# Cross-attention over 98 tiles of keys: the weighted sums of a tile in two groups of four matmuls

## What is computed

```python
lat = layernorm(latents, ...); ctx = layernorm(context, ...)
q = lat @ Wq; k, v = split(ctx @ Wkv)            # 16 heads of 64
attn = clip(einsum("bhnd,bhsd->bhns", q, k) * 64 ** -0.5, -11, 11)
attn = softmax(attn)
out = einsum("bhns,bhsd->bhnd", attn, v) @ Wo + bo
x = x + out
```

## Time and profile before

| | us |
|---|---|
| median of 3 runs | 1075.84 (1074.86 to 1076.63) |
| profiled execution, device time | 1071.72 |
| its span, first to last instruction | 1070.0 |
| PE busy | 1059.8 (99%) |
| PEld busy | 901.2 (84%) |
| DVE busy | 928.6 (87%) |
| ACT busy | 660.9 (62%) |
| POOL busy | 173.0 (16%) |
| chain that ended last | PE 97%, DVE 2% |

### The profile page before, as it was taken

How to read it: one execution, slowest core, us unless ns; L and a number is a source line. 1 busy time by engine, 2 the same in 40 slices (tenths; PEclk the granted TensorE clock), 3 DMA queues, 4 the chain that set the end, 5 groups by cost and what they waited for, 6 DMA issues and landing times.

```text
span 1070.0 us, 18208 instructions
## 1 busy us (share of the span) xinstructions
PE 1059.8 (99%) x5494; PEld 901.2 (84%) x5494; DVE 928.6 (87%) x1326; ACT 660.9 (62%) x934; POOL 173.0 (16%) x213
## 2 busy tenths in 40 slices
PE   9999999999999999999999999999999999999997
PEld 7888888888888888888888888888888888888876
DVE  4999999999999999989888888888888888888875
ACT  4666666666666666656666666666666666666642
POOL 3233232232332332312000000000000000000000
PEclk9999999999999999999999999999999999999998
DMA  5321221222212212231151111111111111111000
GB/s 202 94 73 51 74 65 58 74 51 71 74 49 74 74 49 74 62 98 43 50 124 34 40 44 30 44 44 30 44 44 29 44 43 30 44 30 31 1 1 6
DMA packets 52509, 58.78 MB, mean 55 GB/s; under 512 B 31170, under 2 KB 32772, under 8 KB 52356
## 3 DMA queue, kind: packets, MB, share of 16 engines
q1 hardware_dynamic: 52052, 57.80, 18.7%
q10 hardware_dynamic: 432, 0.66, 0.2%
HBM read 58.20 MB, written 0.13 MB: 55 GB/s over the span
## 4 chain that ended last, share of the span: by engine, by line
PE 97%; DVE 2%; ACT 0%; issue 0%; POOL 0%; DVEq 0%; POOLq 0%
PE wide L457 25%; PE wide L458 25%; PE wide L459 25%; PE wide L498 17%; PE wide L521 1%; PE wide L528 1%; PE wide L535 1%; PE wide L550 0%; PE wide L556 0%; PE wide L543 0%; PE wide L508 0%; PE wide L747 0%; DVE a_max L1222 0%; PE wide L680 0%; PE wide L685 0%
## 5 line engine op out<-in xcount | busy, mean ns | idle before, releaser
L819 ACT ACTIVATE ex<-wide,c_rstd 128x512 f32<-128x512 f32 x392 | 270.3, 689 | 200.7 <-PE wide L459 199.8
L457 PE MATMUL wide<-qk_hi,d_hi 128*128 128x512 f32 x784 | 305.2, 389 | 0.0
L459 PE MATMUL wide<-qk_hi,d_lo 128*128 128x512 f32 x784 | 305.1, 389 | 0.0
L458 PE MATMUL wide<-qk_lo,d_hi 128*128 128x512 f32 x784 | 305.0, 389 | 0.0
L1028 DVE TENSOR_TENSOR ph<-ex,ph 128x1024 fp32r<-128x1024 f32 x195 | 238.9, 1225 | 71.3 <-ACT ph L826 71.1
L826 ACT CAST ph<-ex 128x1024 fp32r<-128x1024 f32 x195 | 205.4, 1053 | 150.1 <-DVE ex L1003 150.1
L1037 DVE TENSOR_TENSOR den_all<-den_all,ex 128x1024 f32<-128x1024 f32 x193 | 234.7, 1216 | 0.0
L498 PEld LDWEIGHTS wide<-ph,vhl 128*128 128x128 f32 x1568 | 212.6, 190 | 16.7 <-DVE ph L1028 2.1
L498 PE MATMUL wide<-ph,vhl 128*128 128x256 f32 x1568 | 219.0, 282 | 0.0
L457 PEld LDWEIGHTS wide<-qk_hi,d_hi 128*128 128x128 f32 x784 | 147.2, 188 | 31.8 <-DVE qk_lo L1042 0.3
L459 PEld LDWEIGHTS wide<-qk_hi,d_lo 128*128 128x128 f32 x784 | 147.1, 188 | 30.6
(11 more groups left out here) (156 smaller groups left out, 628.5 us busy)
## 6 DMA issues: line engine op xcount, KB each, us to landing
t_all<-in_ctxT_dram SPq DMA_DIRECT2D x98, 384.0 KB, 3.1
x_pair<-in_ctx_dram SPq DMA_DIRECT2D x49, 256.0 KB, 2.7
diff<-sig_all SPq DMA_DIRECT2D x194, 0.5 KB, 1.9
wkv<-in_Wo_dram SPq DMA_DIRECT2D x2, 1024.0 KB, 10.0
wq<-in_Wq_dram SPq DMA_DIRECT2D x2, 512.0 KB, 7.3
wkv<-in_Wv_dram SPq DMA_DIRECT2D x2, 512.0 KB, 6.1
wkv<-in_Wk_dram ACTq DMA_DIRECT2D x1, 512.0 KB, 4.7
wkv<-in_Wk_dram SPq DMA_DIRECT2D x1, 512.0 KB, 10.2
```

The costliest lines, as they stand in the source:

```text
L457: pe.matmul(dst, hi, mhi, start=start, stop=False)
L458: pe.matmul(dst, hi, mlo, start=False, stop=False)
L459: return pe.matmul(dst, lo, mhi, start=False, stop=stop)
L819: act.activation(ex[b][:, c * HC:(c + 1) * HC, :], sc_bank[c][:, :].rearrange("p (h q) -> p h q", h=HC), ACT.Exp, scale=c_rstd[s4][:, b:b ...
```

## The change

`weighted_sum` is cut in two. `first_sums` does accumulators 0 and 1 (four matmuls) behind the scores, where all eight stood. `other_sums` does accumulators 2 and 3 of the same tile one iteration later, behind the values of the tile after next and ahead of its scores. `s_pv` is raised by `other_sums`. The last tile has `last_sums` with all eight. At the start of pass two, ACT's copies of the accumulators stand behind `p_high` instead of ahead, DVE's additions behind `p_low`, and the first sums wait for all four saves at once.

```diff
-            def weighted_sum(gp, b, start, stop, saved=0, ended=False):
-
-                g = 2 * gp + b
-                if not ended:
-                    pe.wait_ge(s_plo, g + 1)
-                pe.wait_ge(s_vlo, g + 1)
-                for m in range(MH):
-                    if ended and m % CM == 0:
-                        pe.wait_ge(s_plo, g + 1 + m // CM)
-                    if saved:
-                        pe.wait_ge(s_save, saved - MH + m + 1)
+            def sums(b, start, stop, ms):
+
+                for m in ms:
                     for a in range(2):
                         ins = pe.matmul(acc[m][:, a, :, :], vhl[b][:, 2 * m + a, :, :].rearrange("p n d -> p (n d)"),
                                         ph[b][:, place(m, a), :, :], start=start and a == 0, stop=stop and a == 1)
-                    if ended:
-                        ins.then_inc(s_acc, 1)
-                if not ended:
-                    ins.then_inc(s_pv, 1)
+                return ins
+
+            def first_sums(gp, b, start, stop, saved=0):
+
+                g = 2 * gp + b
+                pe.wait_ge(s_plo, g + 1)
+                pe.wait_ge(s_vlo, g + 1)
+                if saved:
+                    pe.wait_ge(s_save, saved)
+                sums(b, start, stop, CHUNK_M[0])
+
+            def other_sums(b, start, stop):
+
+                sums(b, start, stop, CHUNK_M[1]).then_inc(s_pv, 1)
+
+            def last_sums(b):
+
+                for c in range(CH):
+                    pe.wait_ge(s_plo, ALL + c)
+                    for m in CHUNK_M[c]:
+                        sums(b, False, True, (m,)).then_inc(s_acc, 1)
...
+                    begun = first and p == 0
                     if not ended:
                         values(next_p, gp + b, slot(p, phase, b, 2), 1 - b)
+                    if not begun:
+                        other_sums(1 - b, static and i == 0 and b == 1, static and i == 0 and b == 0)
+                    if not ended:
                         for c in range(CH):
                             scores(next_p, gp + b, slot(p, phase, b, 2), 1 - b, c)
-                    if ended:
+                        first_sums(gp, b, first, last, saved=p * MH if first else 0)
+                    else:
                         pe.wait_ge(s_late, LATE)
                         weights_plain(0, True)
                         pe.wait_ge(s_vlo, ALL)
                         pe.wait_ge(s_den, ALL)
                         denominators(v_bank, den[1], 0)
-                    weighted_sum(gp, b, first, last, saved=p * MH if first else 0, ended=ended)
-                    if ended:
+                        last_sums(b)
...
-                    if static and p > 0 and i == 0 and b == 0:
-                        save_part(p - 1)
                     if more1:
                         p_high(g, b, used=not begun)
                     else:
                         p_high_last(g, b)
+                    if static and p > 0 and i == 0 and b == 0:
+                        save_part(p - 1)
...
-                    if static and p > 0 and i == 0 and b == 0:
-                        save(p - 1)
...
                         p_low_last(g, b)
                         add_den_last(1)
+                    if static and p > 0 and i == 0 and b == 0:
+                        save(p - 1)
```

## The result

The changed kernel takes 1079.74 us (median of 14 runs, 1076.72 to 1082.5) against 1075.49 before (14 runs): a ratio of 1.0044, 95% interval 1.0032 to 1.0056. It is slower by 4.7 us, 3.4 to 6.0. The forecast was 1076.7, no difference; the measured time lies inside the stated range, but on the side and at the price of rival 1 (1080.1 at 0.02 us a tile), and its distance of 4.7 us is beyond the 2.15 us that the prediction took for "no difference".

A forecast was written before the change was run, and what follows sets the result against it. TensorE was taken as the bound, VectorE close behind in the first pass. Terms 0 + 0.2 + 0.7 + 0 = +0.9 us gave 1072.6 on the profiled execution, 1076.7 on the median's scale; range 1073.8 to 1080.6.

The forecast's parts named there:

- rival 1: TensorE, every tile: each switch of matmul group costs its own price; +4.3 us at 0.02 a tile, up to +5.7; chance 0.14.
- part 1: TensorE's work per tile: nothing added or removed, two groups of four sums cost what one of eight does; 0, ±0.03 a tile.
- the prediction's own sign: Prediction is wrong if the distance from S to S in the second pass changes, or the boundary gap is missing.
- S: The group of twelve score matmuls of a tile on TensorE; the clock on which the prediction compared both orders.
- W: The group of all eight sums of a tile on TensorE, in the kernel before the change; 0.95 us.
- rival 3: TensorE, mostly second pass: groups of four leave no trail, 98 x 0.03 = -2.6 us there, -2.0 in all; chance 0.09.
- Part 2: ScalarE's v_high copy waits for O, 0.48 us later past the value matmuls; hidden as before, cost 0.
- O: After the change, the group of the other four sums, of the tile before, on TensorE ahead of S.
- Part 3: Value matmuls come 0.48 us earlier against VectorE's v_low; first pass pays 0.18 once, +0.2 us, second pass 0.
- Part 4: Pass boundary: first sums wait for all four additions, +0.60 us, then values for v_low, another 0.1; +0.7, bounds 0.4 to 1.4.
- Part 5: Start, side steps and last iteration: cost 0; 0.5 us if O were late in the last iteration.

## Why the prediction was right and wrong

The measured time falls into the range, and that is luck: the range had been drawn as far as the middle price of rival 1, while the forecast of no difference (0.76) stood on part 1. By the prediction's own sign it is wrong, since from S to S in the second pass isn't what it was, 5.08 for 5.06.

**Part 1, the work itself: wrong, and the step that failed.** I saw the trail of 0.03 us behind W and asked the right question, what a group of four pays. The answer was read from a row that doesn't carry it: behind W and 16 one-column matmuls the trail is longer than behind W alone, and I took the length for the reason. But those 16 are of another width, and width changes the trail (0.04 us behind 384 columns, 0.03 behind 320, 0.07 behind 128), while length from 1 to 16 doesn't. The row also leaves out the first step behind them, which is the slow one: values and scores start at 955.09 and 956.56, and the next sums at 959.30, 4.21 us for eighteen matmuls instead of 4.08, a trail of 0.13. The term that I put at 0 is 3.9 us. Rival 1 had the mechanism; its top price of 0.03 counted the trail and not the 0.007 us that each short group gains at its first step, so 0.02 is the net one. (Its 5.3 for 196 tiles, like the 2.6 of rival 3 for 98, is 0.027 a tile; with the 0.03 that is printed it would be 5.9.) Its chance, 0.14, was too small for a question on which no row decided.

**Part 2, v_high behind O: right.** S, the exponentials and the clip keep their distance but for the trail: in the second pass the clip starts 3.67 us behind the first of its scores, before 3.64.

**Part 3, the values' wait in pass one: the forecast of 0.2 didn't come.** It was made for a PE at 5.06. At 5.08, 40.64 us for eight tiles, PE is slower than the 40.57 to 40.59 to which DVE holds the kernel before late in pass one, and the margin isn't eaten at all: at 46 us v_low ends 46.05 and the values load at 46.45, 0.40 to spare; at 208 us it is 208.58 and 209.01, 0.43, where 0.48 - 0.48 would leave nothing. No load waited for DVE between 60 and 440 us, and the stall of the kernel before is gone as well, 0.3 us given back. I had this relief in rival 1.

```profile
207.84 0.74 DVE L1005 SCALAR_TENSOR_TENSOR vhl<-wide,c_rstd,vhl 128x512 fp32r<-128x512 f32 x1
...
209.01 0.19 PEld L457 LDWEIGHTS wide<-wv_hi,d_hi 128*128 128x128 f32 x1
```

That it would be paid once only isn't shown; the kernel with all sums behind the values paid in every loop.

**Part 4, the boundary: right, mechanism and size.** 0.60 for the additions and 0.1 for the values were forecast, 0.7 in all; 0.43 and 0.18 came, 0.61. The two kernels on its waits moved the gap as the chain of part 4 says. One term was too small: it let a load follow its releaser by 0.05 us, and here both loads followed by 0.12.

**Part 5: right as far as the trace shows.** Start, side steps and end kept their work; the end differs by the clock.

The rule of the Trainium skill (TensorE: Matmul & The Clock Gate, "Wait — 56ns, not 53.3ns?"), a fixed cost for each matmul on top of N / 2.4 GHz, would have given 0 for part 1. The runs here disagree with it for this kind of operand: a matmul of 512 columns takes 0.227 us behind its like, and twelve of them take 0.027 more in all behind a shorter one.

## What to carry to other kernels

Where TensorE is the bound, count how often it goes from narrow matmuls to wide ones: from 256 to 512 columns each time cost 0.02 us here, whatever the length of the narrow group, so splitting a group adds a cost and merging groups takes one away. Read the distance between starts, not the busy time, and don't take the price of a short group from a row whose matmuls differ in two ways. And where a wait in front of the bound engine is relaxed, look at what stands in the same queue behind the work that it waited for: at this boundary it ended last by nearly the same amount.

## What the runs showed of the hardware

A group of 256-column matmuls between 512-column ones slows the next five, and a single one does it as well (2.75 us for the twelve behind it). The starts behind O in the changed kernel are 602.93, 603.16, 603.40, 603.63, 603.86, 604.09, 604.32, so 1.39 us for six instead of 1.36. Behind 384 columns the slow stretch costs 0.04 us, more than behind 256 or 320 (0.03). The reason isn't settled. A change of bank alone doesn't do it: behind four 512-column matmuls into another bank the twelve take 2.72.
